# Fused decoder on one core: the expert choice moved up in the recurrent program, mixture 2's front reordered, result stores queued six pairs behind the loads, GpSimd's indirect DMAs paced by the up products

## The reference

```
x = _layernorm(x + _L0_attn_ref(x, ...))     # self attention, 16 heads, rotary
x = _layernorm(x + _L0_xattn_ref(x, ctx))    # cross attention on 64 context rows
x = _layernorm(x + _L0_ffn_ref(x, ...))      # mixture 1: 8 experts, top 2, one shared
x = _layernorm(x + _L1_attn_ref(x, ...))     # recurrence over time ("rwkv")
x = _layernorm(x + _L1_xattn_ref(x, ctx))    # single-head cross attention
x = _layernorm(x + _L1_ffn_ref(x, ...))      # mixture 2: 16 experts, top 4, shared
```

## Time and profile before

| | us |
|---|---|
| median of three runs | 1376.79 (1370.61 to 1378.01) |
| profiled execution | 1360.66 |
| its span, first to last instruction | 1358.9 |
| TensorE busy | 1165.4 (86%) |
| VectorE busy | 715.5 (53%) |
| ScalarE busy | 585.8 (43%) |
| GpSimd busy | 501.6 (37%) |

### The profile page before, as it was taken

How to read it: one execution, slowest core, us unless ns; L and a number is a source line. 1 busy time by engine, 2 the same in 40 slices (tenths; PEclk the granted TensorE clock), 3 DMA queues, 4 the chain that set the end, 5 groups by cost and what they waited for, 6 DMA issues and landing times. The chain is left out here.

```text
span 1358.9 us, 23999 instructions
## 1 busy us (share of the span) xinstructions
PE 1165.4 (86%) x7558; PEld 839.3 (62%) x7558; DVE 715.5 (53%) x1906; ACT 585.8 (43%) x1064; POOL 501.6 (37%) x924
## 2 busy tenths in 40 slices
PE   7589899899877967999999999995988676999970
PEld 3244344444344434889999999884555555998850
DVE  4767567676444644423223223285776636655564
ACT  1257677777765643223233233233333122556710
POOL 6333312331421331013333323112321278838856
PEclk9579999999998998999999999997999677999995
DMA  3980000000000007401111111032500024767633
GB/s 139 313 320 2 1 0 0 1 0 0 2 0 1 1 1 283 156 24 40 33 39 40 36 37 39 25 125 74 192 1 0 5 74 139 233 196 213 213 117 101
DMA packets 68127, 109.31 MB, mean 80 GB/s; under 512 B 7345, under 2 KB 54962, under 8 KB 65202
## 3 DMA queue, kind: packets, MB, share of 16 engines
q1 hardware_dynamic: 58130, 80.96, 17.4%
q0 software_dynamic: 9888, 27.01, 6.2%
HBM read 65.61 MB, written 42.34 MB: 79 GB/s over the span
## 5 line engine op out<-in xcount | busy, mean ns | idle before, releaser
L1391 ACT ACTIVATE f_work<-f_bank,f_ub 128x128 f32<-128x128 f32 x312 | 89.0, 368 | 204.3 <-PE f_bank L1713 204.3
L494 ACT ACTIVATE att_PT<-att_ST 128x1024 f32<-128x1024 f32 (+1 forms) x192 | 147.8, 809 | 66.3 <-PE att_ST L608 34.8
L527 DVE CUSTOM_DVE_ANT_0 att_junk<-att_RB,att_causal_q 128x128 f32<-128x128 f32 (+3 forms) x256 | 120.9, 487 | 60.7 <-PE att_RB L590 48.7
L1713 PEld LDWEIGHTS f_bank<-f_work,f_xTf 128*128 128x128 f32 x1248 | 145.4, 192 | 3.9 <-DVE f_work L1513 2.0
L1713 PE MATMUL f_bank<-f_work,f_xTf 128*128 128x128 f32 x1248 | 145.9, 276 | 1.5 <-DVE f_work L1513 1.5
L590 PE MATMUL att_RB<-att_kT,att_qT 96*128 96x512 bf16 (+3 forms) x384 | 122.0, 357 | 23.3 <-DVE att_mx L527 7.2
L1722 PE MATMUL f_bank<-wd_down,f_work 128*128 x624 | 141.2, 380 | 0.0
L1722 PEld LDWEIGHTS f_bank<-wd_down,f_work 128*128 128x128 f32 x624 | 115.8, 191 | 13.8
L1342 POOL DMA_INDIRECT Yd<-f_work,f_inv x39 | 38.5, 987 | 196.3 <-DVE f_work L1532 196.3
L1522 DVE COPY f_xTf<-wu_up 128x1024 f32 x78 | 54.1, 694 | 102.8 <-PE f_bank L1713 95.0
L590 PEld LDWEIGHTS att_RB<-att_kT,att_qT 96*128 96x128 bf16 x384 | 34.0, 99 | 115.9 <-issue 40.4
(11 more groups left out here) (456 smaller groups left out, 2230.9 us busy)
## 6 DMA issues: line engine op xcount, KB each, us to landing
Xd<-g_zero SPq DMA_DIRECT2D x1, 12032.0 KB, 38.4
...
```

What stands on the lines that cost most here:

```text
L494: act.activation(buf[:, :, 0:w], ST[:, 2 * (k % 2):2 * (k % 2) + 2, 0:w], ACT.Exp, scale=float(HD) ** -0.5).then_inc(exp_done, 1)
L527: dve.tensor_tensor_reduce(junk[:, k % RING, 0:w], RB[:, bank, 0:w], G.causal_q[:, 512 - w:512], 1.0, LOWEST, ALU.add, ALU.max, to).then_i ...
L1391: last = act.activation(hT[:, u % 2, m, :], bank[:, UB + m // 4, (m % 4) * P:(m % 4 + 1) * P], ACT.Gelu, bias=ub[:, ds(e, 1), m])
L1713: mm = pe.matmul(bank[:, UB + n, P * m:P * (m + 1)], staged_up[:, kk, at:at + P], xT[:, u % 2, kk, :], start=(kk == 0), stop=(kk == KD - 1))
```

## The change

The recurrent plan puts the choice for half 0 earlier: the transposes for it right behind tx (2, 1), the logits and the four parts of the choice behind v (3, 1), the count behind r (3, 1), `locate` and three scatters behind rs (3, 1), and ten more scatters behind y (3, 1). In mixture 2, GpSimd begins with scatter 13 (`SENT = 13`). On TensorE `count` stands ahead of `shared_down(0)`, the waits for `sh_added` and `pos_ready` ahead of the loop are gone, and `shared_down(1)` stands behind the first two `turn_x`; `down(0)` and `down(1)` wait for the shared sums instead. VectorE and ScalarE stage the weights of the first three pairs ahead of the choice and of the shared expert; `owners(1)`, `shared_sum(1)` and the first two `take_x` change places, and `weights_of` moves into the loop (q = 4 and 6). SyncE stores the result of pair q - 6 behind load q, where it was q - 4 (there are four load buffers as before). GpSimd's pauses are 16 columns wide everywhere; two scatters of half 1 are let go for each `up_ready`, and two gathers of half 0 likewise.

```diff
--- before.py
+++ after.py
@@ -1805,12 +1805,11 @@
         at = plan.index(step) + 1
         plan[at:at] = new
 
-    put(("r", 3, 1), ("tg", 0, 0), ("tg", 0, 1), ("tg", 1, 0), ("tg", 1, 1), ("lg", 0, 0))
-    put(("rs", 3, 1), ("c", 0, 0))
-    put(("y", 3, 1), ("c", 0, 1))
-    put(("tx", 3, 1), ("c", 0, 2))
-    put(("s", 3, 0), ("c", 0, 3), ("ct", 0, 0))
-    put(("dn", 3, 0), ("lc", 0, 0), ("sx", 0, 2))
+    put(("tx", 2, 1), ("tg", 0, 0), ("tg", 0, 1), ("tg", 1, 0), ("tg", 1, 1))
+    put(("v", 3, 1), ("lg", 0, 0), ("c", 0, 0), ("c", 0, 1), ("c", 0, 2), ("c", 0, 3))
+    put(("r", 3, 1), ("ct", 0, 0))
+    put(("rs", 3, 1), ("lc", 0, 0), ("sx", 0, 3))
+    put(("y", 3, 1), ("sx", 3, 13))
     return plan
 
 
@@ -2439,7 +2438,7 @@
     STORES = [[len(range(p, q + 1, 2)) for p in range(2)] for q in LAST]
     NX = 4
     NG = NT // J
-    SCATTERS, SENT = TH * K, 2
+    SCATTERS, SENT = TH * K, 13
     FIRST = NG // 2
     CE = TH * E
     Xd, Yd = a["Xd1"], a["Yd1"]
@@ -2508,11 +2507,12 @@
                 sp.dma_start(Yd[2 * P * q:2 * P * (q + 1), :].rearrange("(i p) c -> p i c", p=P), yo[:, q % 2, :, :]
                              ).then_inc(stored[q % 2], 16)
 
-            for q in range(N + NX):
+            LAG = 6
+            for q in range(N + LAG):
                 if q < N:
                     load(q)
-                if q >= NX:
-                    keep_result(q - NX)
+                if q >= LAG:
+                    keep_result(q - LAG)
             for n, (t0, t1) in enumerate(NORMS):
                 sp.wait_ge(normed, n + 1)
                 sp.dma_start(out_rows[:, t0:t1, :], acc[:, t0:t1, :]).then_inc(out_stored, 16)
@@ -2523,7 +2523,10 @@
             ch = Chain(pool, c_pool)
             pool.memset(half[:, :], -0.5)
             route.scatter(pool, ch, G, Xd, 0, SENT, SCATTERS, route.rest[:, 0:16])
-            route.scatter(pool, ch, G, Xd, 1, 0, SCATTERS, route.rest[:, :])
+            for m in range(0, SCATTERS, 2):
+                if m:
+                    pool.wait_ge(up_ready, m // 2)
+                route.scatter(pool, ch, G, Xd, 1, m, m + 2, route.rest[:, 0:16])
 
             def spread(n):
                 t0, t1 = NORMS[n]
@@ -2538,9 +2541,11 @@
                     if n:
                         pool.wait_ge(weighed, s + 1)
                     for r in range(K):
+                        if n == 0 and r % 2 == 0:
+                            pool.wait_ge(up_ready, LAST[0] + 2 + (K * s + r) // 2)
                         pool.indirect_dma_start(ga[:, s, r, :], None, Yd[0:P * R * (n + 1), :],
                                                 bass.IndirectOffsetOnAxis(pos[:, n, r, s:s + 1], 0)).then_inc(gathered[s], 16)
-                        ch.pause(route.rest[:, 0:16] if n else route.rest[:, :])
+                        ch.pause(route.rest[:, 0:16])
                     if n and s == 0:
                         spread(1)
                     if n and s == 5:
@@ -2575,10 +2580,10 @@
                     act.activation(staged[:, q % 3, i, :], W.all[:, ds(e, 1), :].rearrange("p o f -> p (o f)"), ACT.Copy
                                    ).then_inc(staged_in[i] if q < LATE or i == 0 else staged_late, 1)
 
+            for q in range(3):
+                stage(q)
             for m in range(2 * FIRST):
                 shared_silu(m)
-            for q in range(3):
-                stage(q)
 
             def silu(q):
                 p = q % 2
@@ -2630,17 +2635,6 @@
                 dve.wait_ge(turned[1], i - FIRST + 1)
                 dve.tensor_copy(xTf[:, 1, 512 * i:512 * (i + 1)], bank[:, XB + 2 * (i % 2) + 1, :]).then_inc(copied[1], 1)
             route.owners(dve, ch, 0)
-            dve.wait_ge(exp_done, 1)
-            for m in range(2 * FIRST):
-                shared_product(m)
-                route.choose(dve, ch, 1, m)
-            shared_sum(0)
-            dve.wait_ge(sums_ready, 1)
-            route.locate(dve, ch, 1, bank[:, SB_ + 1, 0:CE], bank[:, SB_ + 1, CE:2 * CE])
-            route.owners(dve, ch, 1)
-            shared_sum(1)
-            for n in range(HALVES):
-                route.weights_of(dve, ch, n)
 
             def take_x(q):
                 p = q % 2
@@ -2694,8 +2688,22 @@
 
             for q in range(3):
                 stage(q)
+            dve.wait_ge(exp_done, 1)
+            route.choose(dve, ch, 1, 0)
+            route.choose(dve, ch, 1, 1)
+            shared_product(0)
+            route.choose(dve, ch, 1, 2)
+            shared_product(1)
+            route.choose(dve, ch, 1, 3)
+            shared_product(2)
+            dve.wait_ge(sums_ready, 1)
+            route.locate(dve, ch, 1, bank[:, SB_ + 1, 0:CE], bank[:, SB_ + 1, CE:2 * CE])
+            shared_sum(0)
+            shared_product(3)
             take_x(0)
             take_x(1)
+            shared_sum(1)
+            route.owners(dve, ch, 1)
             FROM = [LAST[0] + 7 + at for at in (0, 3, 5, 8, 11, 13, 15)]
             when = {FROM[s] + part: (s, part) for s in range(TH - 1) for part in range(2)}
             for q in range(N):
@@ -2704,6 +2712,8 @@
                     take_x(q + 2)
                 if q and q + 2 < LATE:
                     stage(q + 2)
+                if q in (4, 6):
+                    route.weights_of(dve, ch, (q - 4) // 2)
                 if q in when:
                     s, part = when[q]
                     weigh(0, s, 2 * part)
@@ -2812,6 +2822,8 @@
                 pe.wait_ge(ht_done, q + 1)
                 if q >= 2:
                     pe.wait_ge(y_done, q - 1)
+                else:
+                    pe.wait_ge(sh_added, 2 * (FIRST - 1) + q + 1)
                 for i in range(2):
                     mm = pe.matmul(bank[:, YB + p, i * D:(i + 1) * D], hT[:, p, i, :], staged_down[:, q % 3, i, :],
                                    start=True, stop=True)
@@ -2823,16 +2835,13 @@
             shared_up(0)
             shared_up(1)
             shared_up(2)
+            count()
             shared_down(0)
             shared_up(3)
-            count()
-            shared_down(1)
             pe.wait_ge(sh_prod, 2 * FIRST)
-            pe.wait_ge(sh_added, 2 * FIRST)
-            pe.wait_ge(pos_ready, 2)
-
             turn_x(0)
             turn_x(1)
+            shared_down(1)
             up(0)
             turn_x(2)
             for q in range(1, N):
```

## The result

The changed kernel takes 1340.74 us in the median (1338.04 to 1343.06), the kernel before in the same comparison 1374.31 (1370.61 to 1378.01). The ratio is 0.9754, 95% interval 0.9725 to 0.9783: 33.6 us less, where 20.0 less were forecast, 1356.8. A later comparison gave 1348.31 against 1376.99, ratio 0.9786 (0.9765 to 0.9807), 28.7 less.

What follows compares the result with a forecast made beforehand. It took scatters to bound mixture 2's front and TensorE, with load stalls, its loop. Recurrent program +1.6, front -13.4 and loop -8.2 gave -20.0, from 1376.8 to 1356.8 us; own range 1350 to 1363, overall 1342 to 1369.

Steps and rivals of the forecast that it cites:

- The front, -13.4: Mixture 2's start to up(1): 19 scatters instead of 30 cut it from 52.7 to 39.3 us; bounds 9.9 and 14.2.
- I take the difference over as it is.: Sum: the profile's unexplained 16.1 us below the median was kept unchanged, so 1376.8 - 20.0 = 1356.8 us.
- The rival that used the missing 16 us: Timed runs hold longer load stalls than the profile, and the longer lead removes part: -30, 1347 us, chance 0.08.
- The recurrent program, +1.6: Ahead of mixture 2: moving the choice and locate earlier costs 6.3 us, 4.7 come back at the end; bounds -2, +7.
- The loop, -8.25: Mixture 2's pairs: storing q - 6 behind load q lengthens the load lead, so all 8.25 us of stalls go.
- Each is a wait for a load: Loop before the change: all 8.25 us of TensorE stalls were said to be waits for loads.
- Both cost nothing: Loop: paced scatters of half 1 and gathers of half 0, 1.41 us each, were said to add no time.
- The cover that I gave for them: Loop: scatters land 5 us before load(23) would be issued, tile sums gain slack; DMA work 2.7 to 2.8 of 3.09 us.
- The tail: Last down product to the end: 61.7 us before, gathers' number, order and pauses unchanged, so 61 to 62 us expected.
- Staging copies: VectorE's weight copies in the loop: from 1038 ns to near 561 beside narrow pauses, with no time gained.
- The slower case: Loop: DMA engines fill up with two scatters or gathers per pair; +10 in all, 1387 us, chance 0.05.

Runs made afterwards that it cites:

- before_plan_only: Kernel before with only the recurrent plan's part of the change: choice moved up, 13 scatters sent ahead, 19 left to mixture 2; 1358.2 us, ratio 0.989.
- after_more_scatters: Changed kernel with 11 extra scatters, to Yd, ahead of the 19 in mixture 2's front; 1361.33 us, ratio 0.9914.
- after_middle_pauses: Changed kernel with 256-column pauses behind half 0's gathers and half 1's scatters in the loop, instead of 16; 1339.17 us, ratio 0.982.
- before_again: Kernel before, unchanged, for a second profile and the spread of its own time; 1374.72 us, ratio 1.0003.
- before_lag6: Kernel before with only the store changed: pair q - 6 instead of q - 4 behind load q; 1367.36 us, ratio 0.9961.
- before_third: Kernel before, unchanged, on one chip with the changed kernel and the one with 256-column pauses; 1375.47 us, ratio 0.9992.
- before_stage_early: Kernel before with ScalarE's three stage(q) ahead of the four shared silus, nothing else; 1373.38 us, ratio 1.0.

## Why the prediction was wrong

- **The front, -13.4.** The new front was right to 0.4 us, and so was the cause, 11 scatters fewer. What failed is the number subtracted from, 52.7. In ordinary runs of before the front takes 63.6 and 67.7, so the change gains 24 to 26. The scatters were said to bound the front and TensorE to wait 10 us behind; in those runs the fourth silu and what follows it on VectorE bound it. The missed 13.6 us are mostly this: moving 11 scatters away also ended the run of dense scatters beside which the silu was late, shown by before_plan_only, after_more_scatters and the two kernels that only break or slow the scatters.
- **"I take the difference over as it is."** This is the step that failed, in the prediction's words. The profiled execution lay 16 us below the median and 10 below the fastest of the timed ones, so it was no sample of them, and a difference taken from it holds only if the missing 16 us don't lie where the change works; 10.9 of them do. Inside its own condition the sum was good. Between the complete profiles before and after_middle_pauses (the changed kernel but for the pauses in the loop) the recurrent program goes from 60.5 to 60.6, the front from 52.7 to 39.9, the loop from 146.7 to 138.5, the rest stays at 65.8: -20.9 where -20.0 were forecast. The medians of that comparison differ by 24.0. The rival that used the missing 16 us put them into the loads' waits, at 0.08; its time of 1347 was the nearest, its reason fell with before_again and before_lag6.
- **The recurrent program, +1.6.** Against the first profile it is +1.7. Against before_again it is -1.6, since that profile has the r (3) projection at half clock (+3.0), and before_third and before_stage_early too, while the changed kernel has it so in any case (6.35 us). The forecast sum was right by its own profile and the sign wrong for these.
- **The loop, -8.25.** The mechanism was right: the lag of 6 takes all waits for loads away. "Each is a wait for a load" was too much, though: in the first profile TensorE is idle for 4.9 of the 8.25 us, and the rest is its lower clock after the waits. The size was wrong, as -2.6 came of it. "Both cost nothing", said of scatters and gathers at 1.4 us, is the step that failed here: with gathers at 1.57 or 2.0 the loop of the changed kernel has 138.5 to 140.3, at 1.37 144.1 to 145.2 (142.8 and 143.3 in the two kernels with 30 scatters in the front). The cover that I gave for them (DMA share, slack of the sums) was true and not what they cost. Whether they cost anything in a complete trace is not shown.
- **The tail.** 61.7, as forecast. What I had not seen is that it depends on when half 0's gathers end, by the drain.
- **Staging copies.** VectorE's took 581 ns in the mean of 23 between 1135 and 1205 us, near the 561 forecast and below 1038. The Trainium skill's warning (SBUF — State Buffer, "SBUF: two separate sides"), that such copies keep GpSimd from writing its descriptors, cost no time here: two scatters of a pair come 1.37 to 1.73 us apart beside these copies, where 1.37 is their pace in the front, and no load waits for them.
- **The slower case** (DMA engines filling up) did not come: from 1140 to 1280 the DMA share is 0.69.

The sum by stretches, before_again to after: recurrent -1.6, front -23.9, loop -2.6, rest +0.5, together -27.6, near the 28.7 of the last comparison. The 33.6 of the first holds some 6 more; in the two traces 4.2 of it are the first stretch, which the change doesn't touch. The rest stays unexplained. How much of the front's gain is a gain of the kernel, and how much one of its recorded executions, stays open too, as long as no run shows it without recording.
